# Squaring the next x chunk on VectorE instead of GpSimd in a fused RWKV attention and gated FFN kernel

## The reference

```
xn  = (x - mean(x)) / sqrt(var(x) + 1e-5)            # over the 1024 channels
k   = xn @ Wk.T ;  r = xn @ Wr.T ;  v = r
y_t = (a + exp(u + k_t) * v_t) / (b + exp(u + k_t))  # a, b: sums over the past,
a   = exp(w) * a + exp(k_t) * v_t                    # decayed by exp(w), w = -exp(time_decay),
b   = exp(w) * b + exp(k_t)                          # u = time_first
att = (sigmoid(r) * y) @ Wo.T
ffn = (silu(xn @ Wg.T) * (xn @ Wu.T)) @ Wd.T         # 3072 hidden, int weights / 127
out = x + att + ffn
```

## Time and profile before

| | us |
|---|---|
| the two runs | 1987.5 and 2145.12, median 2066.31 |
| the profiled execution | 1988.26 |
| its span, slowest core (core 0) | 1986.7 |
| its spans, all cores | 1972.3 to 1986.7 |
| first program on core 0, until SP issues the first FFN weight load | 877.9 |
| first matmul of the second program on core 0 | 942.3 |
| PE / DVE / ACT / POOL busy on core 0 | 1473.0 / 805.5 / 363.4 / 73.7 |

### The profile page before, as it was taken

The page is one execution under the profiler, slowest core; times in us unless marked ns, Lnnn a source line. Parts: engine busy times, 40 slices in busy tenths (PEclk is TensorE's granted clock), DMA queues, the critical chain, the costliest instruction groups (busy, mean ns, idle before and its releaser), DMA issues.

```text
span 1986.7 us, 17678 instructions; the slowest of 8 cores (1972.3 to 1986.7 us)
## 1 busy us (share of the span) xinstructions
PE 1473.0 (74%) x6368; PEld 630.3 (32%) x6368; DVE 805.5 (41%) x1325; ACT 363.4 (18%) x621; POOL 73.7 (4%) x49
## 2 busy tenths in 40 slices
PE   2628373655637374630999999999999999999997
PEld 0203030212212121210444444444444444444443
DVE  5686768686868686830111111111111111111111
ACT  0323232231414141400110101101101011010110
POOL 0010100001010100000000000000000000000000
PEclk8769686777869696865999999999999999999998
DMA  9901808080716210149002002011020020300201
GB/s 196 139 4 26 144 14 156 0 160 10 113 57 98 72 64 0 64 134 334 18 1 105 1 22 85 1 64 43 22 85 1 21 85 1 106 1 22 85 1 43
DMA packets 47108, 129.05 MB, mean 65 GB/s; under 512 B 1392, under 2 KB 9584, under 8 KB 46448
## 3 DMA queue, kind: packets, MB, share of 16 engines
q0 software_dynamic: 14512, 67.11, 16.5%
q1 hardware_dynamic: 32512, 60.83, 9.4%
HBM read 111.16 MB, written 60.82 MB: 87 GB/s over the span
## 4 chain that ended last, share of the span: by engine, by line
PE 51%; SPq 2%; DMA 1%; DVE 1%; issue 0%; DVEq 0%; POOL 0%; POOLq 0%
PE psB_gu L642 17%; PE psB_gu L653 17%; PE psB_d L687 9%; PE psB_d L669 8%; DMA xnb<-xn_scr 1%; DVE pb L602 1%; SPq L563 1%; SPq L571 0%; PE psB_d L676 0%; SPq L559 0%; SPq L567 0%; DVE pb L609 0%; POOL out_cm L698 0%; DVEq L546 0%; SPq L555 0%
## 5 line engine op out<-in xcount | busy, mean ns | idle before, releaser
L595 DVE SCALAR_TENSOR_TENSOR h_act<-psB_gu,silu 128x512 bf16<-128x512 f32 x192 | 132.8, 692 | 747.9 <-PE psB_gu L653 747.9
L642 PE MATMUL psB_gu<-xnb,wgbf 128*128 128x512 bf16 x1536 | 364.6, 380 | 75.8 <-DMA xnb<-xn_scr 75.8
L653 PE MATMUL psB_gu<-xnb,wubf 128*128 128x512 bf16 x1536 | 363.5, 380 | 0.0
L624 ACT ACTIVATE silu<-psB_gu 128x512 f32<-128x512 f32 x192 | 114.6, 597 | 884.8 <-PE psB_gu L642 884.8
L642 PEld LDWEIGHTS psB_gu<-xnb,wgbf 128*128 128x128 bf16 x1536 | 150.6, 98 | 258.2 <-issue 78.0
L653 PEld LDWEIGHTS psB_gu<-xnb,wubf 128*128 128x128 bf16 x1536 | 150.5, 98 | 182.0 <-issue 1.4
L687 PE MATMUL psB_d<-h_act,wdbf 128*128 128x512 bf16 x768 | 177.2, 395 | 22.5 <-DVE pb L602 22.5
L669 PE MATMUL psB_d<-h_act,wdbf 128*128 128x512 bf16 x736 | 188.9, 379 | 0.0
L418 PE MATMUL ps_wo<-outpre,wo_bf 128*128 128x512 bf16 x448 | 116.4, 419 | 97.0 <-DVE xn_buf L376 82.7
L434 PE MATMUL ps_k<-xn_buf,wk_bf 128*128 128x512 bf16 x512 | 135.2, 412 | 46.2 <-ACT k_sb L175 26.2
L443 PE MATMUL ps_r<-xn_buf,wr_bf 128*128 128x512 bf16 x512 | 125.7, 390 | 0.0
(11 more groups left out here) (117 smaller groups left out, 958.3 us busy)
## 6 DMA issues: line engine op xcount, KB each, us to landing
x_buf<-x_cm SPq DMA_DIRECT2D x8, 2048.0 KB, 34.0
pt_scr<-x_buf POOLq DMA_DIRECT2D x8, 2048.0 KB, 12.3
pb<-pt_scr SPq DMA_DIRECT2D x8, 2048.0 KB, 8.9
out_cm<-pb POOLq DMA_DIRECT2D x8, 2048.0 KB, 7.5
xn_scr<-xn_buf POOLq DMA_DIRECT2D x8, 1024.0 KB, 41.1
xnb<-xn_scr SPq DMA_DIRECT2D x8, 1024.0 KB, 5.4
wg_bfd<-wgT POOLq DMA_DIRECT2D x4, 1536.0 KB, 54.8
wu_bfd<-wuT POOLq DMA_DIRECT2D x4, 1536.0 KB, 32.1
```

The costliest lines, as they stand in the source:

```text
L595: ve.scalar_tensor_tensor(out=h_act[:, hg * TC:(hg + 1) * TC], in0=up_sl(hg), scalar=1.0 / 127.0, in1=silu[hg % 2], op0=Alu.mult, op1=Alu. ...
L624: sc.activation(out=silu[hg % 2], in_=gate_sl(hg), func=Act.Silu, scale=1.0 / 127.0).then_inc(sem["s_sil"], 1)
L642: ins = te.matmul(gate_sl(hg), wgbf[:, gc * HID + hg * D:gc * HID + (hg + 1) * D], gsl(xnb, gc), start=(gc == 0), stop=(gc == G - 1))
L653: ins = te.matmul(up_sl(hg), wubf[:, gc * HID + hg * D:gc * HID + (hg + 1) * D], gsl(xnb, gc), start=(gc == 0), stop=(gc == G - 1))
```

## The change

The six squarings of chunks 2 to 7 move from GpSimd's program to VectorE's. On VectorE the squaring of chunk j+2 stands at the end of chunk j, behind the normalisation of chunk j+1 (L376) and ahead of the first residual additions and scans of chunk j+1. VectorE gets two of the three waits that stood before it on GpSimd: x of chunk j+2 has landed, and the DMA of xn of chunk j out of that buffer has ended. The third, for t_rog, is left out. GpSimd's waits there go, too, so that it goes from issuing the DMA of xn (L504) straight to the wait for the residuals (v_res). Instruction, tiles and types stay the same, as does the semaphore for PE (v_sq).

```diff
@@ vector
                         ve.tensor_sub(gsl(xn_buf[q1], G - 1), xtmp[G - 1],
                                       msb_sb).then_inc(sem["v_xn"], 1)
+                    if j + 2 < NCH:
+                        ve.wait_ge(*sa_x(j + 2))
+                        ve.wait_ge(*g_xn_done(j))
+                        ve.tensor_mul(xn_buf[(j + 2) % 2], x_buf[(j + 2) % 3],
+                                      x_buf[(j + 2) % 3]).then_inc(sem["v_sq"], 1)
@@ gpsimd
                     ).then_inc(sem[f"g_xn{j % 2}"], 16)
-                    if j + 2 < NCH:
-                        gp.wait_ge(*sa_x(j + 2))
-                        gp.wait_ge(*g_xn_done(j))
-                        gp.wait_ge(sem["t_rog"], 8 * j + 8)
-                        gp.tensor_mul(xn_buf[(j + 2) % 2], x_buf[(j + 2) % 3],
-                                      x_buf[(j + 2) % 3]).then_inc(sem["v_sq"], 1)
                     gp.wait_ge(sem["v_res"], 8 * j + 8)
```

## The result

The changed kernel takes 1958.4 us (median of 7 runs) against 1987.4 (median of 6 runs of the kernel before, most of them made together with it; the median of 2066.3 given ahead of the prediction lay midway between runs of 1987.5 and 2145.1). The ratio is 0.985, with a 95% interval of 0.984 to 0.987: 1.5% faster, under the 2% line. Every ratio here leaves out the runs in which the cores of a die were slowed at a lower granted clock. The forecast was 1958 and 1.5%.

What follows compares the result with a forecast made beforehand. VectorE was taken to set the first program's pace, stopped by GpSimd's six multiplies. Core 2, last after the gains, at 1956.3 plus 1.6 outside its span gave 1957.9 us, 1.5% under 1988.3; own range 1950 to 1968, whole 1946 to 1972.

Steps and rivals of the forecast that it cites:

- The stop: GpSimd's multiply halts VectorE until it ends; removal saves 6.53 us in chunk 0, 6.66 in chunk 2, 3.80 in the last.
- The free pace: Period between L376 starts with no multiply in it, taken as 98.9 us from core 0's last chunk; six make 593.4.
- Chunk 0: L306 no longer stopped; of 6.53 us, 1.5 become L336's wait for PE and 5.1 are gained.
- The cores: Gain per core is last minus first L376, less 593.4, plus 5.1: core 0 36.3 us, core 2 28.7, core 5 30.9.
- The hidden multiply: VectorE's six added multiplies of 4.43 us behind L376 fall into its waits; first L325 0.4 late, cost on the path 0.
- Rival B: The multiply is not hidden on VectorE behind L376; 26.6 us come back, 1984.5 us, no change; 8%.
- The waits: VectorE's added waits for x and the xn copy cost nothing; 10.6 us are left in chunk 1.
- Rival D: VectorE blocks waiting for x of chunk j+2, priced once the load lands over 10.6 us later; slower; 3%.
- Rival A: Each GpSimd multiply costs every core its full length, 42.4 us in all; 1945.9 us, 2.1% faster; 12%.
- Rival C: The landing x load causes VectorE's stop, the multiply merely follows the same event; stop stays, 1988 us; 3%.

Runs made afterwards that it cites:

- Run 1: Kernel before, squaring still on GpSimd but with one more wait so it starts only behind L376 of the same chunk; 1954.1 us against 1984.4, ratio 0.985.
- run 2: Changed kernel, squaring moved up on VectorE between the eight L372 and the subtractions, ahead of PE's release; 1979.5 us against 1984.4, ratio 0.9975.
- run 7: Changed kernel, x loads of chunks 3 to 7 held back until L376 of the chunk in which they are squared; 1994.5 us, ratio 1.003.
- run 5: Changed kernel, x loads of chunks 3 to 7 held back until VectorE's scan of group 7 two chunks earlier; 1955.7 us, ratio 0.986.
- run 3: Changed kernel plus a GpSimd memset of the same tile at the multiply's old place, overwritten by VectorE's multiply; 1956.7 us, ratio 0.986.

## Why the prediction was right, step by step

*The stop.* Right in kind and price. Every stretched line is back at its normal length. On core 0 the five stops inside the periods had lengthened single VectorE instructions by 4.5, 6.7, 6.8, 6.0 and 3.8 us, 27.8 together, and its six periods are now 29.2 us shorter. Run 1 shows that it is the multiply's place and not its existence that costs. A GpSimd instruction that reads SBUF holds, until its own end, the next VectorE instruction with two SBUF inputs, and the tensor-scalar L361 with one; L325 and L354 pass. On core 1 of the kernel before, the last multiply lay over the eight maxima, which read one SBUF input and took their usual 4.84 us, and held only what came behind them:

```profile
645.75 7.00 POOL L512 TENSOR_TENSOR xn_buf<-x_buf 128x4096 bf16<-128x4096 f32 x1 [39.41 <-DMA x_buf<-x_cm]
...
645.35 4.84 DVE L354 TENSOR_REDUCE Mall<-k_sb 128x1 f32<-128x512 f32 x8 [0.16 <-issue]
650.27 2.51 DVE L357 TENSOR_TENSOR t1b<-Mall,relu_u 128x8 f32<-128x8 f32 x1
```

*The free pace.* 98.9 us was a little low; 99.2 to 99.3 came, some 2 us over six chunks. In core 3's trace the first two periods are 99.8 and 99.6, the next three 99.0 and the last 99.3.

*Chunk 0.* L336 was to wait about 1.5 us for PE once L306 is no longer held:

```profile
108.61 0.68 DVE L336 TENSOR_SCALAR rows<-psA_st 1x512 f32<-1x512 f32 x1 [1.64 <-PE psA_st L400]
```

It waits 1.64.

*The cores.* The gain of the kernel was to be less than core 0's, and it was: core 0 came from 1986.7 to 1950.0 (1950.4 forecast), the kernel from 1986.7 to 1957.1. The other cores do not bear the rule out. Core 2 ended at 1951.1 (1956.3 forecast) and core 5 at 1947.7 (1953.6). Cores 3 and 4, which I had left aside, came last with 1957.1 and 1956.8, where the same rule gives 1950.8 and 1945.5. The rule held two things fixed that move between executions. One is the first L376: 148.1, 149.6 and 148.2 were forecast on cores 0, 2 and 5, and 145.3, 146.2 and 143.0 came; on core 3 it was 148.8, later than its old start less the 5.1. The other is the stretch from the last L376 to the end: 1213.3 us before and 1209.2 now on core 2, 1212.0 and 1209.0 on core 5, 1210.4 and 1212.7 on core 3. On core 2 it makes 4.1 of the 5.2 us. It is not the second program, which takes 1042.8 to 1045.0 us on every core of both traces, but what lies between the two; why it moves was not looked into. So it is partly luck that 1958 is right to the microsecond: single cores were off by up to 11 us, the maximum over eight was not. The mean is sounder: the eight spans fell by 29.2 us in the mean, and the rule gives 31.2.

*The hidden multiply.* 5.1 us behind L376 was forecast for the first L325, 5.06 measured; 12.3 for the scan, 12.57 measured. Rival B's price of 26.6 us is borne out by run 2 (24.2, within its interval), its condition is not met; its estimate that the cover ends about 10 us behind L376 fits the 10.4 of run 7.

*The waits.* 10.6 us of distance between the landing and the multiply were forecast for chunk 1. The load goes out at 200.23 on core 3 and takes 37.1 us, to 237.3, against 249.18: 11.9. Rival D's rule, nothing lost up to that distance and the full price beyond it, was never tested in its first half, since the loads of run 5 landed as early as before. The second half counts too much: in run 7 core 0 waits 41.4 us in its five chunks and its six periods are 32.9 us longer than in the changed kernel. The rule left out both the cover, which takes up about half of each wait, and the slower clock, which adds to the loss. And the distance in issue time is larger than thought, because a later load is a faster one.

*Rival A* (full length, 42.4 us) did not come: a hit costs only from where the stopped instruction was due, and less where a wait follows, as argued. *Rival C* is refuted by run 1, where the loads land as before and nothing is stretched.

## What to carry to other kernels

An engine that looks idle can still stop the busiest one: where a short instruction of the pacing engine takes forty times its usual length and ends with another engine's instruction, price the time lost there as critical work. Before moving work, try moving its start into a wait of the pacing engine; here one semaphore wait on GpSimd was worth as much as the whole change, and leaves the pacing engine's queue free of a wait for a DMA. Do not read such a gain off the slowest core alone: core 0 gained 36.7 us, the mean of the eight cores 29.2 and the kernel 29.6. Which core comes last changes from execution to execution (core 3, 5, 3, 0, 0 and 4 in six of the changed kernel), so a forecast for a single core can miss by ten microseconds where the mean holds.

## What the runs showed of the hardware that I had not expected

- VectorE's L325, with one input in SBUF and one in PSUM, runs at its usual 0.69 us inside a 7.0 us GpSimd multiply (run 1), while a 128x8 tensor-scalar instruction with its input in SBUF is held for 6.83 us. The maxima L354, 128x512 with one input in SBUF, take their usual 4.84 us for eight inside a multiply (core 1 of the kernel before).
- A GpSimd memset, which reads nothing, lets two tensor-tensor instructions pass at 0.17 us and holds a 128x8 tensor-scalar one for 2.04 us, to its own end (run 3).
- The same 2 MB load takes 36 us in the median issued early and 12 issued some 25 us later, and lands at nearly the same time (run 5). Beside GpSimd's DMAs it moved 0.15 MB in 24 us, with 73 packets against their 95, which carried 2.59 MB.
- A wait of 3.83 us on PE cost 6.3: the granted clock went from 1.00 to 0.50, and the 16 matmuls behind the wait took 6.11 us in place of 3.62 (run 7).
